# A graph network kernel on one core: a re-ordered set-up that loads the first pass, and two TensorE signals per group in the message stage

## The reference

```python
Wxh = x @ Wl.T + bl
h = silu(rbf @ Wf1.T + bf1)
f_ij = h @ Wf2.T + bf2
msg = f_ij * Wxh[j]                       # j: dst of an edge
agg = segment_sum(msg, i, n)              # i: src of an edge
x = layernorm(x + (layernorm(x + agg) * gamma + beta))
msg = x[src] * edge_weight[:, None]
agg = segment_sum(msg, dst, n)
x = layernorm(x + relu((agg + x) @ W1 + b1) @ W2 + b2)
```

## Time and profile before

| | us |
|---|---|
| median of 3 runs | 3303.69 |
| lowest and highest run | 3300.82, 3312.31 |
| the profiled execution's own time | 3301.68 |
| its span, first to last instruction | 3299.7 |

### The profile page before, as it was taken

How to read it: one execution, slowest core, us unless ns; L and a number is a source line. 1 busy time by engine, 2 the same in 40 slices (tenths; PEclk the granted TensorE clock), 3 DMA queues, 4 the chain that set the end, 5 groups by cost and what they waited for, 6 DMA issues and landing times. The chain is left out here.

```text
span 3299.7 us, 57203 instructions
## 1 busy us (share of the span) xinstructions
PE 2051.3 (62%) x18002; PEld 1373.3 (42%) x18002; DVE 2563.1 (78%) x4987; ACT 1001.9 (30%) x2288; POOL 2335.0 (71%) x2177
## 2 busy tenths in 40 slices
PE   2655565656555556666676666663783666658886
PEld 2222222222222233333444444443773655547775
DVE  6877777777777777778787787774875999978887
ACT  3222222222222222222222222221676666641001
POOL 0677777777777777777777777774234888868775
PEclk8888878787887788888888888886755677769999
DMA  7743445333333334444444445434654999989997
GB/s 199 196 124 124 124 124 150 95 95 94 94 95 93 95 116 127 127 135 138 134 142 144 143 151 153 147 98 139 194 166 152 354 363 358 357 324 405 395 392 286
DMA packets 261217, 605.85 MB, mean 184 GB/s; under 512 B 112847, under 2 KB 130127, under 8 KB 248375
## 3 DMA queue, kind: packets, MB, share of 16 engines
q1 hardware_dynamic: 186330, 385.45, 38.1%
q0 software_dynamic: 67488, 210.15, 17.3%
q10 hardware_dynamic: 7205, 7.74, 0.9%
HBM read 403.92 MB, written 199.25 MB: 183 GB/s over the span
## 5 line engine op out<-in xcount | busy, mean ns | idle before, releaser
L1332 POOL DMA_INDIRECT region_rows<-x_space,pos x1664 | 1657.4, 996 | 531.4 <-issue 504.2
L1128 PE MATMUL ps_cnt<-ident,work 128*128 128x128 f32 x832 | 178.2, 353 | 760.2 <-DVE work L1228 760.2
L1035 ACT CAST x_space<-ps_cnt 128x512 bf16<-128x512 f32 x208 | 121.7, 585 | 1461.9 <-PE ps_cnt L1128 1461.9
L1128 PEld LDWEIGHTS ps_cnt<-ident,work 128*128 128x128 f32 x832 | 116.6, 176 | 931.2 <-issue 931.2
L1217 DVE TENSOR_REDUCE rank<-work 128x8 f32<-128x784 f32 x208 | 323.4, 1555 | 21.8 <-DVE work L1213 0.5
L1121 PE MATMUL ps_fx<-work,w_wf 128*128 128x512 f32 x416 | 253.6, 694 | 67.6 <-ACT work L1026 66.7
L1233 DVE TENSOR_TENSOR work<-ps_cnt,x_space 128x512 f32<-128x512 f32 x208 | 143.8, 691 | 124.8 <-ACT x_space L1035 124.8
L1091 PE MATMUL ps_th<-x_space,w_wf 128*128 128x512 f32 x416 | 220.4, 613 | 9.4 <-DMA x_space<-rbf 9.4
L1114 PE MATMUL ps_fx<-work,x_space 128*64 128x512 bf16 x1248 | 225.3, 478 | 0.0
L1213 DVE TENSOR_TENSOR work<-onehot,ps_rank 128x784 f32<-128x784 bf16 x208 | 201.9, 971 | 7.2
L1197 DVE COPY x_space<-edges_space 128x16 f32 (+1 forms) x208 | 39.8, 191 | 212.5 <-DMA region_rows<-x_space,pos 212.0
(11 more groups left out here) (276 smaller groups left out, 5322.1 us busy)
## 6 DMA issues: line engine op xcount, KB each, us to landing
tmp_space<-key_rows SPq DMA_DIRECT2D x98, 576.0 KB, 7.7
x_space<-rbf SPq DMA_DIRECT2D x104, 512.0 KB, 3.8
tmp_space<-rel_rows SPq DMA_DIRECT2D x104, 512.0 KB, 4.1
region_rows<-x_space,pos POOLq DMA_INDIRECT x1664
tmp_space<-region_rows SPq DMA_DIRECT2D x48, 441.0 KB, 4.1
tmp_space<-region_rows SPq DMA_DIRECT2D x25, 588.0 KB, 5.1
region_rows<-x_space SPq DMA_DIRECT2D x12, 1176.0 KB, 7.2
tmp_space<-region_rows SPq DMA_DIRECT2D x25, 539.0 KB, 4.5
```

The source lines that it names most:

```text
L1128: last = e.transpose(ps_cnt[:, t * P:(t + 1) * P], product[:, t * P:(t + 1) * P], ident[:, :])
L1332: e.indirect_dma_start(out=region_rows, out_offset=bass.IndirectOffsetOnAxis(ap=pos[j][:, t:t + 1], axis=0), in_=rows_f[j][:, t, :], in_of ...
```

## The change

**The set-up.**
- Partition p of a set of 8 blocks now holds the 8 consecutive nodes 8p to 8p+7 instead of node p of each block: the host lays `x_t` out that way, and `part_rows` and `wxh_rows` are written in pieces of 8 nodes (3072 and 2048 bytes).
- ScalarE issues only the weights that Wxh needs, then the node loads; the other eleven weights go one per set. SP issues its large loads once the first node load has landed.
- VectorE's work on indices and group ends stands between the sets of the loop (`ends_of_groups` after set 1, and so on), constants ahead of it. From set 5 on the subtraction of the high part is done by POOL (`subtract_high`, NEAR_RESTS = 5), with four buffers instead of two, as are the casts of src to hi and lo.
- SP loads what pass 0 of the message stage needs while the set-up runs: edge features, `rel_rows` and `near`. It loads only passes from 1 on in the message stage (LOADED = 1). The fills of the regions' tails come last on SP instead of first.

**The message stage.** `blocks` and `early_sums` don't signal any more. What waited for `rk` or `e_mm` now waits for `xw`, the last product of `nodes`; `bk` and `xw` are left, two signals per group. The order of instructions within the stage is the same on every engine.

```diff
@@ set_up, gpsimd @@
+                    e.wait_ge(src_d, 1)
+                    e.tensor_copy(hi_s[:, :], shifted_s).then_inc(src_split, 1)
+                    e.wait_ge(src_d, 2)
+                    e.tensor_copy(lo_s[:, :], src_i).then_inc(src_split, 1)
+                    for g in range(NEAR_RESTS, GN):
+                        subtract_high(e, g).then_inc(w_r1_far, 1)
...
@@ set_up, sync @@
+                    for u in range(S // BATCH):
+                        e.dma_start(found[S + u], rbf_batches[u, :, :]).then_inc(ld[u], 16)
+                    for g in range(GN):
...
+                        if g == UNDER + 4:
+                            e.wait_ge(r_out, 16)
+                            e.wait_ge(w_under, 16 * UNDER)
+                            for u in range(S // BATCH):
+                                e.dma_start(rel_b[u], rel_batches[u:u + 1, :].broadcast_to([P, width])).then_inc(rl[u], 16)
+                        e.wait_ge(w_lo, g + 1)
+                        e.dma_start(part_rows[g * T * P:(g + 1) * T * P, :].rearrange("(p t) w -> p (t w)", t=T),
+                                    wxh[:, wxh_blocks(g), :, :].rearrange("p t c d -> p (t c d)")
+                                    ).then_inc(w_under if g < UNDER else w_parts, 16)
+                    e.wait_ge(s_base, 1)
+                    e.wait_ge(w_parts, 16 * (GN - UNDER))
+                    for j in range(S):
+                        node = e.value_load(base_i[0:1, j:j + 1], min_val=0, max_val=(NB - 1) * P)
+                        e.dma_start(near[j], part_rows[bass.ds(node, P), :]).then_inc(nl[j], 16)
...
@@ set_up, vector @@
+                    e.wait_ge(w_ab, 32)
+                    for g in range(GN + 3):
                         if g < GN:
                             add(g)
-                        if 0 <= g - 1 < GN:
-                            rest_part(g - 1)
-                        if 0 <= g - 2 < GN:
-                            low_part(g - 2)
+                        if 0 <= g - 1 < NEAR_RESTS:
+                            subtract_high(e, g - 1).then_inc(w_r1, 1)
+                        if 0 <= g - 3 < GN:
+                            low_part(g - 3)
+                        if g == 1:
+                            ends_of_groups()
+                        if g == 2:
+                            relative_rows()
...
@@ sorted_messages, tensor: blocks @@
-                        last = e.matmul(ps_pairs[0:NB, NB * TQ:PAIRS], block_of_octet[j % 2][:, 1, :], moved[:, tiles(i, j)],
-                                        start=False, stop=False)
-                        last.then_inc(rk, 1)
+                        e.matmul(ps_pairs[0:NB, NB * TQ:PAIRS], block_of_octet[j % 2][:, 1, :], moved[:, tiles(i, j)],
+                                 start=False, stop=False)
@@ early_sums @@
-                        last.then_inc(e_mm, 1)
@@ vector: block_onehot, positions, early_onehot, early_total @@
-                        e.wait_ge(rk, count_of(i, j, 1))
+                        e.wait_ge(xw, count_of(i, j, 1))
...
-                        e.wait_ge(rk, count_of(i, j))
+                        e.wait_ge(xw, count_of(i, j))
...
-                        e.wait_ge(e_mm, n.number + S - 1)
...
-                    def early_total(n):
-                        e.wait_ge(e_mm, n.number + S + 1)
+                    def early_total(n, i, j):
+                        e.wait_ge(xw, count_of(i, j))
...
@@ nodes_by_feature @@
-        a = a.reshape(NBP // T, T // 2, 2, P, D).transpose(0, 2, 4, 1, 3)
+        a = a.reshape(NBP // T, P, T // 2, 2, D).transpose(0, 3, 4, 2, 1)
```

More of the change, by code:

```diff
@@ L522, in products @@
                         last.then_inc(w_f, 1)
-                    products(0)
-                    products(1)
+                    for g in range(GN):
+                        products(g)
                     e.wait_ge(s_const, 5)
@@ L528, in _ @@
                     e.matmul(ps_h[:, P:2 * P], ones_f[:, :], diag[:, :], start=True, stop=True).then_inc(s_sum, 1)
-                    for g in range(2, GN):
-                        products(g)
                 @block.vector
@@ new lines, in relative_rows @@
+                    def relative_rows():
+                        e.wait_ge(s_rel, 32)
+                        step(e.tensor_scalar(firsts_f[0:GP, :], firsts_i[0:GP, :], float((NB - 1) * P), None, ALU.min))
+                        for h in range(GH):
+                            group = slice(h * T * P, (h + 1) * T * P)
+                            last = e.tensor_scalar(rel[0:GP, group], dst_rows_i[0:GP, group], firsts_f[0:GP, h:h + 1], None,
+                                                   ALU.subtract)
+                        last.then_inc(s_rel, 1)
@@ L892, in sorted_messages @@
             e_ld = [own(f"e_ld_{u}") for u in range(RING)]
-            e_kc, e_oh, e_mm = (own(f"e_{k}") for k in ("kc", "oh", "mm"))
+            e_kc, e_oh = (own(f"e_{k}") for k in ("kc", "oh"))
             at = width + T * D
@@ L914, in over_passes @@
                         between(lo)
+                    if lo < loaded:
+                        body(lo, k, first)
+                        lo += 1
                     if hi == lo + 1:
@@ L1083, in _ @@
                 def _(e):
-                    seed(e, rk, xw, bk, e_mm)
+                    seed(e, xw, bk)
                     empty = block_iota[:, :, :].rearrange("p n t -> p (n t)")[:, 0:PAIRS]
@@ L1137, in early_sums @@
                             for c in range(PARTS):
-                                last = e.matmul(early_sum, place[:, :, t], rows[:, t, c * D:(c + 1) * D],
-                                                start=(t == 0 and c == 0), stop=(t == n.tiles - 1 and c == PARTS - 1))
-                        last.then_inc(e_mm, 1)
+                                e.matmul(early_sum, place[:, :, t], rows[:, t, c * D:(c + 1) * D],
+                                         start=(t == 0 and c == 0), stop=(t == n.tiles - 1 and c == PARTS - 1))
                     def steady(i, j, left, n):
```

253 lines of the change are left out of this document (146 added, 107 removed).

## The result

The changed kernel takes 3346.19 us (median of 4 runs, 3345.70 to 3352.34) beside 3302.26 us for the kernel before on the same chip: ratio 1.0131, 95% interval 1.0107 to 1.0155. The profiled execution took 3345.7 us, its span is 3343.9 us, 44.2 more than before, where the forecast had 22. That is outside the stated range (3300 to 3342), on the side of the forecast's sign.

What follows compares the result with a forecast made beforehand. POOL's scatter queue was taken to bound the message part. From the profiled 3301.7 us, 20 us for an earlier first scatter came off and 42 us for the signals went on, plus 2 for the median: 3325.7 us, range 3300 to 3342.

Steps and rivals of the forecast that it cites:

- The bound: Message part: POOL's never-starved queue of 1664 scatters, 1.301 us each, 2165 us, sets two thirds of the span.
- The signals: Message stage: VectorE's count read waits for the node products, 57 us of delay less 15 of lead, 42 us slower.
- It is a loop, so 0.76 us is added to each turn of it: Message stage loop: the longer wait at the count read recurs every group, 57 us summed over the stretches.
- with node products at the lower clock in some groups, up to 52: Message stage: upper value for the last scatter's delay, 52 us instead of 42, if some node products run slower.
- Only two edits can change the total there: POOL's scatter queue: only the moment of the first scatter, or making POOL wait later, can move the total.
- The set-up: Before the message stage: VectorE's work falls from 51.6 to 45 us; the stage ends at 55.5 instead of 67, -11.5 us.
- the third rival: Set-up: VectorE is held while POOL subtracts, up to 13 us, using up the 11.5 us gain; 3337 us; chance 0.09.
- at most +1.0: Set-up: cost to VectorE, in us, of the pass over lo_s taken from ScalarE.
- The prologue: Start of the message stage: preloaded edge features save 9.3 us, the moved signal adds 0.75 in the first group.
- The missing signal gives nothing back: TensorE in the message stage: no stall seen from signalling, nothing taken; the skill's price would give an estimated 4 us.
- The marks I set: Changed profile: first scatter near 75 us, POOL idle some 40 us more after about 1700, count-read waits 0.7 us longer.
- The rivals by which the cover holds, wholly or by half: Message loop: slack hides the signal delay, 3284 us, chance 0.13; or delay is 0.5 us a turn, 3302 us, 0.12.

Runs made afterwards that it cites:

- best_more: Changed kernel with rk put back ahead of the pairs matmuls, sixteen idle GpSimd waits, and TensorE's hidden matmul repeated three times more per turn: 3273.91 us, ratio 0.9926.
- rk_counts: Changed kernel with rk put back, but signalled by the last counts matmul, ahead of the three pairs matmuls: 3271.53 us, ratio 0.9921.
- more_work: Changed kernel with TensorE's hidden matmul repeated three times more in each turn: 3284.45 us, ratio 0.9954.
- pool_code: Changed kernel with rk put back and sixteen already met waits added to GpSimd's part of the set-up: 3268.0 us, ratio 0.9914.
- rk_back: Changed kernel with the rk signal of the last pairs matmul and its two waits put back, e_mm still away: 3275.7 us, ratio 0.9927.
- both_back: Changed kernel with both signals and their waits put back, leaving only the new set-up: 3275.38 us, ratio 0.9931.

## Why the prediction was wrong, step by step

**The bound, right.** POOL's queue bounds the message part while it is fed; best_more and rk_counts show that nothing on TensorE matters as long as it is.

**Where the 22 us went.** The span grew by 44.2 us and not by 22. The start won 10.8 us less than forecast (6.9 in the set-up, 3.9 at the first scatter), the signals cost 71 us and not 42, the shorter scatters gave 15.3 us that weren't forecast, and the rest of the program 2.2.

**The signals: right mechanism, mis-sized term; this is the step that failed.** The sentence "It is a loop, so 0.76 us is added to each turn of it" took one group, and one at the upper clock. The turns grow by 0.89, 0.88 and 1.21 us in k1, k2, k3, and by 0.15 in k0: 24 x 0.15 + 24 x 0.89 + 24 x 0.88 + 27 x 1.21 = 79 us, where I had 57. At the upper clock my size about holds: the 46 turns lie 0.44, 0.59 and 0.69 us over before's mean, and 0.43, 0.66 and 0.83 us over before's own turns with fast node products. The other 27 turns are 1.2 to 1.3 us longer still, 33 us in all, on the low clock. I had seen that clock ("with node products at the lower clock in some groups, up to 52") and given it 10 us; it wasn't only the node products that ran on it, and with the clock kept up (more_work) not 33 but 57 us of the price are gone. POOL's lag at the last group is 15.2 us in before and 1.1 now, so 14 us of lead are used up (I took 15): 79 - 14 = 65 us, of which the part shows 55.7, since the shorter scatters made the first 108 groups some 9 us faster (108 x 8 x 10 ns). Against the kernel with the same set-up and both signals the sum closes: the turns grow by 0.24, 0.99, 0.92 and 1.26 us, 86 us in all, less 13.9 of lead is 72, and the two traces differ by 71.

**"Only two edits can change the total there": wrong by 15 us.** I had looked at when POOL may scatter, not at how long a scatter takes. The casts and subtractions on GpSimd shorten each of 1664 scatters by 10 ns. No row of before could show it. It hides a part of the first miss, which is luck: without it the change would have cost some 60 us.

**The set-up: 4.6 us instead of 11.5.** The sum for VectorE was 45 us and it is busy 53.8. Of the 8.8 us, 4.7 are the thirteen last subtractions (1041 instead of 683 ns), 0.8 the five others, 0.95 each the comparison and the pass over lo_s: 7.4 us is the third rival's mechanism, which I had at up to 13 us and gave 0.09. Another 1.0 is the pass over lo_s itself, 2.0 us and not "at most +1.0". What moving the work to GpSimd should have won (7.5 us) is what running beside it took.

That sum isn't yet the 4.6 us. The last rows of the stage in the changed kernel:

```profile
58.69 1.95 DVE L705 SCALAR_TENSOR_TENSOR edges_space<-edges_space,scalars 128x1664 f32<-128x1664 bf16 x1
...
61.42 0.64 SPq L527 DMA_DIRECT2D run_rows<-x_space  x1
```

VectorE is done at 60.6 us; SyncE issues its last fill until 62.07, and TensorE starts 2.65 us later. In pool_code VectorE is done at the same time, SyncE 1.0 us earlier, and TensorE starts 0.8 us earlier. So SyncE ended the stage, as the forecast allowed with its 55.5 us. It came 6.6 us later than that: its last part write was issued at 51.3 us and not at 45, since VectorE's last low part was done only then; landing, node loads and fills took 10.8 us, 10.5 forecast.

**The prologue, right; the first scatter, not.** From TensorE's first matmul to the finished record the sum would be 16.7 us (26.2 less 9.3, plus 0.75, less 0.98 us, since in before the record was done at 94.50 and the scatter started at 95.48); it is 81.36 - 64.71 = 16.65. That it fits so closely is luck: with the same set-up and the old signal it is 16.76 us in rk_back and 15.3 in both_back, so the 0.75 us don't show, and VectorE's wait of 4.09 us in the first group is now for the landing of seed_rows, with 0.28 us left for the node products. Then 4 us were lost to the code load, at a place where I expected only a spare 18 us. The fills did no harm there, but they stood last in SyncE's queue, which ended the set-up.

**The missing signal gives nothing back: right.** e_mm put back or not is the same within the measurement.

**The marks I set.** First scatter after 85 us meant that the set-up sum is wrong: it came at 86.3, and the sum was. POOL first starves at 1615 us, in group 148, earlier than 1700, since k0 and half of k1 used up the lead. The rivals by which the cover holds, wholly or by half, fell with that. L1282's last wait is at 1178 us, where I had 1800. The waits at the read of the counts grew by 0.9, 0.9 and 1.3 us a group, not 0.7. POOL's idle time before its scatters, the first one's left out, grew from 507 to 579 us, by 72 and not by 40; its busy time fell by 16.

## What to carry to other kernels

Price a wait that moves to a later signal by all that runs between the two signals, over many turns and at both clock levels, not by one row; a longer wait elsewhere makes TensorE's pause longer, and the pause lowers the clock for what comes next. Work moved from VectorE to GpSimd gave next to nothing here, because the two worked on SBUF at the same time: read it from the durations of VectorE's neighbours. Before summing one engine's work, ask which engine's queue ends the stage. And where an engine is fed from a queue with a lead, look for gains at its start and in the length of its own instruction; everything else is only cover.

## What the runs showed of the hardware

- A GpSimd that has run a cast in the set-up (in all but one kernel a subtraction too, even of 128x4 elements) issues the indirect scatters in 958 to 959 ns, one that hasn't in 969 to 970 ns: fourteen traces of the one kind and four of the other, no exception.
- GpSimd's code load, one packet of 8192 bytes: where it came between the first finished record and the first scatter (at 84.0 us in the changed kernel), with the other queues busy (shares 59.2% and 47.0%), the scatter came 4.5 to 6.0 us after the record (five traces), otherwise 1.0. Sixteen instructions more moved it ahead (65.0 us), eight subtractions fewer behind (92.5 us).
- TensorE in a pause of 4.5 us: the granted clock fell to 0.50, and the next 5.9 us of matmuls ran at 0.50 and 0.55. In the turn after it, with a pause of 4.1 us, the transposes still ran at the upper level (0.63 us). Redundant matmuls in the pause kept the mean of the stretch at 0.94 instead of 0.80.
- The same kernels took about a fifth longer on another chip, with engines standing still for 10 to 20 us at a time; only instruction durations could be compared there. What held them isn't known.
